# First layer of an adjacency kernel: product with the second weight after the sum over nodes, biases spread by DMA, other queues for x and the first piece of adj

## The chip, the cores and the metric

One core of a Trainium2 chip. TensorE (PE) multiplies, VectorE (DVE), ScalarE (ACT) and GpSimd (POOL) do the elementwise work, SyncE (SP) only issues transfers. SP and ACT each have a DMA queue of their own; q1 is SP's and q10 is ACT's. The metric is the time of one execution on the device in microseconds; less is better.

## The reference

x is 4096 nodes x 128 features, adj is 4096 x 4096, all float32. adj holds no negative value, and few of its entries are not zero.

```
# layer 0: at most 350 entries a row are kept; here no row has more
T    = tanh(adj * adj)                  # where adj > 0
h2   = tanh(x @ W_proj + b_proj)
feat = relu(T @ (h2 @ W_gcn) + b_gcn)
x    = layernorm(x + feat)
# layer 1
pos  = (adj > 0) @ x ;  neg = (adj < 0) @ x
y    = [pos, neg] @ node_weight + node_bias * diag(adj)
y   += (adj @ x) @ edge_weight + edge_bias * diag(adj)
x    = layernorm(x + y)
```

## The kernel before

The eight chunks of a layer are 512 rows of adj each. A chunk has eight halves of 512 columns (four blocks of 128). Each half goes through the same steps: DMA brings it in rows (four quarters make a piece of two halves, 2 MB), DVE transposes it by 32 x 32 squares into a_cols (L581, helper `turn`), and in layer 0 POOL squares three quarters of it (L354), ACT the rest (L515), ACT takes the tanh (L520), and PE adds four products of 128x512 to the accumulator acc (L913). There are four slots for halves; a slot comes free when PE has used it.

The work is written out by hand as one program for each engine, in order, with semaphores between them. Every engine takes its own list strictly in that order.

Ahead of the first chunk stands a head, the list USES, which makes the operand `rhs` = tanh(x W_proj + b_proj) W_gcn of 4096 nodes in eight groups of 512 nodes. A group is a "turn" (PE transposes x, L876, DVE copies it out of PSUM, L591), a "hid" (PE multiplies with W_proj, one product of 128x512, L881; ACT adds the bias and takes the tanh, L483), and a "rhs" (PE multiplies with W_gcn, four products of 128x128, L887; DVE, L593, or ACT, L488, copies it out). The groups are interleaved over six PSUM banks. EARLY names the places of DVE's list in the head at which the first halves of adj are transposed. ACT's list has the eight tanhs ahead of its first square (L515) of adj.

x comes in five parts of 4, 4, 8, 8 and 8 blocks (X_PARTS), each in four quarters of partitions: SP's queue brings the first two quarters of every part (L365), ACT's queue the other two (L457). Both queues have piece 0 of adj between parts 3 and 4. From group 2 on, ACT issues one quarter of the later pieces of adj after each tanh of the head (L460).

After a chunk, ACT empties acc into z_t with bias b_gcn and relu (L496), and PE transposes z_t back to rows (L898, `turn_to_rows`) between the first and second half of the next chunk. DVE adds x (L645) and normalises (L602 to L633), and ACT and POOL split the result in a high and a low part for layer 1.

Layer 1 uses for each block a product with adj (L922) and two with the mask adj > 0 (L923, L924). In its first chunk PE spreads the three bias rows over the partitions by products with a row of ones (L960 to L962) and DVE copies them out (L718).

## Time and profile before

| | us |
|---|---|
| median of three runs (621.15 to 621.41) | 621.28 |
| the profiled execution | 622.29 |
| its span, first to last instruction | 620.5 |
| PE busy in the span | 603.0 |
| DVE busy | 475.7 |
| ACT busy | 415.7 |
| POOL busy | 186.7 |

The span is what the trace covers; the profiled execution's own time has 1.8 us more around it. Its time is 1.0 us above the median of the other runs. Busy times of engines overlap.

### The profile page before, as it was taken

What the parts mean: (1) busy time and instruction counts of PE and PEld (TensorE: products, weight loads), DVE (VectorE), ACT (ScalarE), POOL (GpSimd) and SP (SyncE); (2) the same over time, 40 slices, a digit from 0 to 9 for tenths busy, and PEclk for the clock granted to TensorE, in tenths of its full rate; (3) what the DMA queues carried; (4) which work ended last, traced back from release to release, by engine and by line L of the source; (5) the groups of instructions that cost most, each with busy time, mean ns of one, the idle gap of its engine ahead of it and who ended that gap; (6) DMA issues with size and microseconds to landing.
All of it is one profiled execution on the core that took longest, in us unless ns stands there. A gap on an engine that the chain in (4) does not pass through costs nothing.

```text
span 620.5 us, 5693 instructions
## 1 busy us (share of the span) xinstructions
PE 603.0 (97%) x1966; PEld 342.3 (55%) x1966; DVE 475.7 (77%) x703; ACT 415.7 (67%) x293; POOL 186.7 (30%) x79
## 2 busy tenths in 40 slices
PE   7799999999999999999999999999999999999994
PEld 5544444444444444555655655655655656558993
DVE  2676979788887979986697696796786886877735
ACT  2378686868687686548784883983883874856850
POOL 0387697978879697000000000000000000000000
PEclk9899999999999999999999999999999999999998
DMA  8999999999999980048889398486595684883000
GB/s 235 336 347 347 330 282 315 270 328 287 324 281 298 315 197 0 1 135 229 219 250 252 97 246 232 127 243 188 154 250 154 186 248 125 230 232 96 2 18 18
DMA packets 141181, 130.65 MB, mean 211 GB/s; under 512 B 9443, under 2 KB 141158, under 8 KB 141158
## 3 DMA queue, kind: packets, MB, share of 16 engines
q1 hardware_dynamic: 74982, 66.22, 38.4%
q10 hardware_dynamic: 66176, 64.17, 37.2%
q8 instruction: 9, 0.15, 0.1%
q14 instruction: 14, 0.11, 0.1%
HBM read 128.27 MB, written 2.10 MB: 210 GB/s over the span
## 4 chain that ended last, share of the span: by engine, by line
PE 94%; DMA 2%; ACTq 2%; ACT 1%; DVE 1%; issue 0%
PE acc L913 35%; PE acc L922 33%; PE stage L924 10%; PE stage L923 10%; PE stage L922 2%; DMA x_rows<-in_x_dram 2%; PE to_rows L932 1%; PE to_rows L933 1%; ACTq L457 1%; ACTq L460 1%; PE to_rows L898 1%; PE stage L881 1%; ACT a_cols L520 0%; PE to_cols L887 0%; ACT a_cols L515 0%
## 5 line engine op out<-in xcount | busy, mean ns | idle before, releaser
L581 DVE STREAM_TRANSPOSE a_cols<-a_rows 128x2048 f32<-128x2048 f32 x128 | 294.6, 2306 | 90.8 <-PE stage L924 55.1
L922 PE MATMUL acc<-a_cols,x_rows 128*128 128x512 f32 (+1 forms) x512 | 248.1, 566 | 0.0
L913 PE MATMUL acc<-a_cols,rhs 128*128 128x512 f32 x512 | 221.4, 593 | 1.3 <-ACT a_cols L520 1.3
L923 PE MATMUL stage<-masks,x_hi 128*128 128x512 f32 (+1 forms) x288 | 208.5, 724 | 0.0
L354 POOL TENSOR_TENSOR a_cols<-a_cols 128x1536 f32<-128x1536 f32 x64 | 175.2, 2746 | 63.5 <-DVE a_cols L581 62.9
L913 PEld LDWEIGHTS acc<-a_cols,rhs 128*128 128x128 f32 x512 | 96.6, 190 | 120.4 <-issue 120.4
L520 ACT ACTIVATE a_cols<-a_cols 128x2048 f32<-128x2048 f32 x64 | 122.3, 1912 | 50.6 <-POOL a_cols L354 49.4
L536 ACT ACTIVATE a_rows<-a_rows 128x4096 f32<-128x4096 f32 x32 | 116.0, 3624 | 26.4 <-DVE a_cols L581 13.3
L539 ACT ACTIVATE a_rows<-a_rows 128x4096 f32<-128x4096 f32 x32 | 115.9, 3623 | 1.0
L924 PE MATMUL stage<-masks,x_lo 128*128 128x512 f32 (+1 forms) x288 | 106.7, 370 | 0.0
L922 PEld LDWEIGHTS acc<-a_cols,x_rows 128*128 128x128 f32 x512 | 94.0, 189 | 20.1 <-issue 0.5
L924 PEld LDWEIGHTS stage<-masks,x_lo 128*128 128x128 f32 x288 | 54.5, 189 | 55.4 <-issue 53.7
L923 PEld LDWEIGHTS stage<-masks,x_hi 128*128 128x128 f32 x288 | 54.3, 188 | 55.7 <-issue 53.9
L711 DVE TENSOR_SCALAR masks<-a_cols 128x2048 fp32r<-128x2048 f32 x64 | 79.0, 1234 | 2.2
L548 ACT COPY z_t<-acc 128x512 f32<-128x512 f32 x7 | 4.1, 585 | 65.1 <-PE stage L924 65.1
L515 ACT ACTIVATE a_cols<-a_cols 128x512 f32<-128x512 f32 x64 | 39.6, 618 | 5.9 <-issue 3.7
L922 PE MATMUL stage<-a_cols,x_rows 128*128 128x256 f32 x64 | 19.1, 380 | 0.0
L347 POOL TENSOR_TENSOR x_lo<-x_rows,x_hi 128x512 fp32r<-128x512 f32 x8 | 11.2, 1403 | 22.5 <-ACT x_hi L502 22.5
L483 ACT ACTIVATE early<-stage,b_col 128x512 f32<-128x512 f32 x7 | 4.8, 687 | 16.1 <-PE stage L881 10.0
L661 DVE COPY sm_t<-stage 128x512 f32<-128x512 f32 x7 | 4.8, 691 | 11.6 <-PE stage L924 11.6
L591 DVE COPY early<-stage 128x512 f32<-128x512 f32 x5 | 3.4, 690 | 11.3 <-PE stage L876 11.3
L932 PE MATMUL to_rows<-w_pne,z_t 128*128 128x128 f32 x60 | 11.7, 276 | 0.0
(84 smaller groups left out, 234.1 us busy)
## 6 DMA issues: line engine op xcount, KB each, us to landing
a_rows<-in_adj_dram SPq DMA_DIRECT2D x120, 512.0 KB, 8.9
a_rows<-in_adj_dram ACTq DMA_DIRECT2D x120, 512.0 KB, 10.0
out_dram<-n_rows SPq DMA_DIRECT2D x28, 64.0 KB, 8.4
x_rows<-in_x_dram SPq DMA_DIRECT2D x6, 128.0 KB, 4.2
x_rows<-in_x_dram ACTq DMA_DIRECT2D x6, 128.0 KB, 5.5
x_rows<-in_x_dram SPq DMA_DIRECT2D x4, 64.0 KB, 2.3
x_rows<-in_x_dram ACTq DMA_DIRECT2D x4, 64.0 KB, 2.7
diag<-in_adj_dram SPq DMA_DIRECT2D x16, 1.0 KB
```

Of the source, the lines that this page charges most:

```text
L354: nc.gpsimd.tensor_tensor(part, part, part, ALU.mult).then_inc(squared_pool, 1)
L515: nc.scalar.activation(rest, rest, ACT.Square).then_inc(squared_act, 1)
L520: nc.scalar.activation(a_cols[:, hs, :, :], a_cols[:, hs, :, :], ACT.Tanh)\
L536: nc.scalar.activation(piece, piece, ACT.Sign, accum_out=signs[:, bass.ds(col, 1)])\
L539: nc.scalar.activation(piece, piece, ACT.Relu, scale=-1.0, accum_out=negs[:, bass.ds(col, 1)]).then_inc(counted, 1)
L581: nc.vector.transpose(half_out(hs), half_in(s, h % HALVES)).then_inc(turned[layer], 1)
L711: nc.vector.tensor_scalar(masks[:, hs, :, :], a_cols[:, hs, :, :], 0.0, None, ALU.is_gt)\
L913: last = nc.tensor.matmul(acc[parity][:], rhs[:, b, :], a_cols[:, h % HSLOTS, k, :], start=(b == 0), stop=(b == BLOCKS - 1))
L922: nc.tensor.matmul(sums, x_rows[:, b, :], cols, start=(b == 0), stop=(b == BLOCKS - 1))
L923: nc.tensor.matmul(sums_m, x1_hi[:, b, :], mask, start=(b == 0), stop=False)
L924: return nc.tensor.matmul(sums_m, x1_lo[:, b, :], mask, start=False, stop=(b == BLOCKS - 1))
L932: nc.tensor.matmul(rows[:, k, :], blk(z_t, at + k), w_pne[:, 2, :], start=True, stop=False)
```

## The change

Layer 0 is computed as (T h2) W_gcn in place of T (h2 W_gcn).

- The "rhs" steps of the head go: eight times four products of 128x128, and the copies after them. The operand of the big products is h2 itself.
- The "hid" step changes sides: PE now has the transposed x as the stationary operand and W_proj as the moving one, four products of 128x128 in place of one of 128x512, so that h2 comes out in rows. DVE adds the bias on the way out of PSUM (it lies along the free axis now), and ACT takes the tanh in place in SBUF.
- `turn_to_rows` becomes `project`: the four transposes of z_t by the identity become four products of z_t with W_gcn.
- ACT only copies acc to z_t. The bias b_gcn and the relu move behind the projection, to DVE: one addition, and one maximum with the addition of x.
- All biases come spread over the 128 partitions by DMA. The three bias products of layer 1 and their copy go, and one small addition on DVE is new.
- SP's queue brings all of x but two quarters of part 0, then W_gcn and its bias, and then its half of pieces 1 to 3. ACT's queue brings the four quarters of piece 0 right after its two quarters of x. W_gcn was ACT's.
- EARLY is [("turn", 7), ("hid", 6)]: the first half of adj is transposed ahead of the copy of turn 7, the second ahead of hid 6.

```diff
-    EARLY = [("turn", 7), ("rhs", 4), ("rhs", 6)]
+    EARLY = [("turn", 7), ("hid", 6)]
...
         for k in range(GROUPS):
-            USES += hids[k:k + 1] + rhss[max(k - 2, 0):max(k - 1, 0)] + turns[k + 2:k + 3]
-        USES += rhss[GROUPS - 2:]
+            USES += hids[k:k + 1] + turns[k + 2:k + 3]
...
-            for part in range(1, X_FIRST):
-                load_x(part)
-            load_piece((0, 0), 0)
-            for part in range(X_FIRST, len(X_PARTS)):
-                load_x(part)
+            sp.dma_start(b_proj_bc, b_proj.partition_broadcast(P)).then_inc(proj_loaded, 16)
+            for part in range(1, len(X_PARTS)):
+                load_x(part, range(QUARTERS))
+            sp.dma_start(w_pg[:, 1, :], w_gcn).then_inc(gcn_loaded, 16)
+            sp.dma_start(b_gcn_bc, b_gcn.partition_broadcast(P)).then_inc(gcn_loaded, 16)
...
+            for q in range(QUARTERS):
+                load_quarter((0, 0), 0, q)
+
+            for g in range(GROUPS):
+                act.wait_ge(stage_dve, count_of("hid", g))
+                nc.scalar.activation(h2[:, g * TILES:(g + 1) * TILES, :], h2[:, g * TILES:(g + 1) * TILES, :], ACT.Tanh)\
+                    .then_inc(hid_ready, 1)
+                if g >= 2:
+                    load_quarter((0, 0), g // 2, ACT_QUARTERS[g % 2])
...
-                nc.scalar.activation(by_tile(z_t[:]), by_set(acc[parity][:]), ACT.Relu, bias=b_col[:, 1:2])\
-                    .then_inc(z_ready, 1)
+                nc.scalar.copy(by_tile(z_t[:]), by_set(acc[parity][:])).then_inc(z_ready, 1)
...
+                    nc.vector.tensor_tensor(h2[:, g * TILES:(g + 1) * TILES, :],
+                                            bank_of(n).rearrange("p (b f) -> p b f", f=F), to_all(b_proj_bc, TILES),
+                                            ALU.add).then_inc(stage_dve, 1)
...
-                    nc.vector.tensor_tensor(to_rows[:], to_rows[:], rows, ALU.add).then_inc(y_ready, 1)
+                    nc.vector.tensor_tensor(to_rows[:], to_rows[:], to_all(b_gcn_bc, TILES), ALU.add)\
+                        .then_inc(biased, 1)
+                    dve.wait_ge(biased, c + 1)
+                    nc.vector.scalar_tensor_tensor(out=to_rows[:], in0=to_rows[:], scalar=0.0, in1=rows, op0=ALU.max,
+                                                   op1=ALU.add).then_inc(y_ready, 1)
...
-                    last = nc.tensor.transpose(to_rows[:, k, :], z_t[:, k * P:(k + 1) * P], ident[:])
+                    last = nc.tensor.matmul(to_rows[:, k, :], blk(z_t, k), w_pg[:, 1, :], start=True, stop=True)
...
-                        nc.tensor.matmul(stage[0][:, 0:F], ones[0:1, :], b_row[:, 0, :], start=True, stop=False)
-                        nc.tensor.matmul(stage[0][:, 0:F], ones[0:1, :], b_row[:, 1, :], start=False, stop=True)
-                        nc.tensor.matmul(stage[0][:, F:2 * F], ones[0:1, :], b_row[:, 2, :], start=True, stop=True)\
-                            .then_inc(bias_staged, 1)
```

PE's list before, from turn 6 of the head to the first chunk (early holds the transposed x and the tanh of the hidden layer):

```order
L876 MATMUL stage<-ident,x_rows 128x128 x4
L881 MATMUL stage<-early,w_pg 128x512
L887 MATMUL to_cols<-w_pg,early 128x128 x4
L876 MATMUL to_rows<-ident,x_rows 128x128 x4
L881 MATMUL stage<-early,w_pg 128x512
L887 MATMUL stage<-w_pg,early 128x128 x4
L881 MATMUL stage<-early,w_pg 128x512
L887 MATMUL stage<-w_pg,early 128x128 x4
L887 MATMUL to_cols<-w_pg,early 128x128 x4
L887 MATMUL to_rows<-w_pg,early 128x128 x4
L913 MATMUL acc<-a_cols,rhs 128x512 x32
```

PE's list of the change at the same place (L863 is the turn, L869 the hid):

```order
L863 MATMUL to_rows<-ident,x_rows 128x128 x4
L869 MATMUL stage<-w_pg,feat_t 128x128 x4
L863 MATMUL stage<-ident,x_rows 128x128 x4
L869 MATMUL stage<-w_pg,feat_t 128x128 x8
L897 MATMUL acc<-a_cols,h 128x512 x32
```

The last rows ahead of the big products were four rounds of L887; now they are the two last hids.

DVE's list before, from the copy of turn 6 on:

```order
L591 COPY early<-stage 128x512
L581 STREAM_TRANSPOSE a_cols<-a_rows 128x16x4x32
L591 COPY early<-to_rows 128x512
L581 STREAM_TRANSPOSE a_cols<-a_rows 128x16x4x32
L593 COPY rhs<-stage 128x512 x2
L581 STREAM_TRANSPOSE a_cols<-a_rows 128x16x4x32
L593 COPY rhs<-to_cols 128x512
L593 COPY rhs<-to_rows 128x512
```

DVE's list of the change at the same place (L567 copies a turn, L571 adds the bias to a hid, L559 transposes adj):

```order
L567 COPY feat_t<-to_rows 128x512
L571 TENSOR_TENSOR h<-stage,b_lent 128x512
L559 STREAM_TRANSPOSE a_cols<-a_rows 128x16x4x32
L567 COPY feat_t<-stage 128x512
L559 STREAM_TRANSPOSE a_cols<-a_rows 128x16x4x32
L571 TENSOR_TENSOR h<-stage,b_lent 128x512 x2
L559 STREAM_TRANSPOSE a_cols<-a_rows 128x16x4x32 x11
```

Before, no tanh of the head stood behind a transpose of adj other than through the copy of turn 7; now the additions of hid 6 and 7, from which ACT takes its last two tanhs, stand behind both early transposes.

SP's list before:

```order
L365 DMA x_rows<-in_x_dram 32x4x128 x2
L373 DMA w_pg<-in_L_gnn_W_proj_dram 128x128
L374 DMA b_col<-in_L_gnn_b_proj_dram 128x1
L365 DMA x_rows<-in_x_dram 32x4x128 x2
L365 DMA x_rows<-in_x_dram 32x8x128 x4
L369 DMA a_rows<-in_adj_dram 32x16x256 x2
L365 DMA x_rows<-in_x_dram 32x8x128 x2
L369 DMA a_rows<-in_adj_dram 32x16x256 x62
```

SP's list of the change:

```order
L361 DMA x_rows<-in_x_dram 32x4x128 x2
L370 DMA w_pg<-in_L_gnn_W_proj_dram 128x128
L371 DMA b_lent<-in_L_gnn_b_proj_dram 128x128
L361 DMA x_rows<-in_x_dram 32x4x128 x4
L361 DMA x_rows<-in_x_dram 32x8x128 x12
L374 DMA w_pg<-in_L_gnn_W_gcn_dram 128x128
L375 DMA bias_bc<-in_L_gnn_b_gcn_dram 128x128
L365 DMA a_rows<-in_adj_dram 32x16x256 x62
```

SP now issues twice as many transfers of x, none of them behind a piece of adj.

## Rows read from the trace of the kernel before

**Rows 1.** The page: busy times, and the chain's shares.
```profile
PE 603.0 (97%) x1966; PEld 342.3 (55%) x1966; DVE 475.7 (77%) x703; ACT 415.7 (67%) x293; POOL 186.7 (30%) x79
...
PE acc L913 35%; PE acc L922 33%; PE stage L924 10%; PE stage L923 10%; PE stage L922 2%; DMA x_rows<-in_x_dram 2%; PE to_rows L932 1%; PE to_rows L933 1%; ACTq L457 1%; ACTq L460 1%; PE to_rows L898 1%; PE stage L881 1%; ACT a_cols L520 0%
```

**Rows 2.** The chain that ended last, 0 to 64 us: start, us, what.
```profile
7.66 12.36 DMA x_rows<-in_x_dram
...
24.63 0.86 PE stage L881 x2
25.49 0.89 PE stage L887 x8
...
32.88 1.92 ACT a_cols L520
...
34.93 27.70 PE acc L913 x64
62.64 0.44 PE to_rows L898 x4
```

**Rows 3.** The timeline, 0 to 45 us: start, us, engine, line, operation, idle before.
```profile
20.16 0.63 PE L876 MATMUL stage<-ident,x_rows 128*128 128x128 f32 x4 [2.90 <-DMA x_rows<-in_x_dram]
...
20.82 0.69 DVE L591 COPY early<-stage 128x512 f32<-128x512 f32 x1 [2.83 <-PE stage L876]
...
21.43 2.30 DVE L581 STREAM_TRANSPOSE a_cols<-a_rows 128x2048 f32<-128x2048 f32 x1
...
22.29 0.69 ACT L483 ACTIVATE early<-stage,b_col 128x512 f32<-128x512 f32 x1 [5.20 <-PE stage L881]
...
23.82 2.75 POOL L354 TENSOR_TENSOR a_cols<-a_cols 128x1536 f32<-128x1536 f32 x1 [22.20 <-DVE a_cols L581]
...
27.86 0.62 ACT L515 ACTIVATE a_cols<-a_cols 128x512 f32<-128x512 f32 x1
...
28.52 1.91 ACT L520 ACTIVATE a_cols<-a_cols 128x2048 f32<-128x2048 f32 x1
28.52 3.64 ACTq L460 DMA_DIRECT2D a_rows<-in_adj_dram  x2
...
30.57 3.67 PE L913 MATMUL acc<-a_cols,rhs 128*128 128x512 f32 x8 [0.65 <-ACT a_cols L520]
```

**Rows 4.** DMA from 6 to 8 us: queue, packets, MB, share of 16 engines.
```profile
q1 hardware_dynamic: 549, 0.27, 49.4%
q10 hardware_dynamic: 514, 0.25, 45.7%
```

**Rows 5.** The same from 16 to 18 us.
```profile
q1 hardware_dynamic: 499, 0.32, 60.6%
q10 hardware_dynamic: 495, 0.28, 55.2%
```

**Rows 6.** The same from 20 to 22 us.
```profile
q1 hardware_dynamic: 349, 0.35, 55.0%
```

**Rows 7.** The same from 10 to 12 us.
```profile
q1 hardware_dynamic: 280, 0.28, 57.3%
```

**Rows 8.** Stretches: us, busy of PE, PEld, DVE, ACT, POOL, then granted clock, DMA, GB/s.
```profile
20.00:25.00 5.00, 4.84 (x20) 3.74 (x21) 3.24 (x3) 1.27 (x2) 1.19 (x1) 0.66 1.10 348
```

**Rows 9.** The timeline around the three bias products of layer 1.
```profile
263.86 0.40 PE L924 MATMUL stage<-masks,x_lo 128*128 128x512 f32 x1
...
264.09 1.02 PE L922 MATMUL acc<-a_cols,x_rows 128*128 128x512 f32 x2
...
265.18 0.40 PE L924 MATMUL stage<-masks,x_lo 128*128 128x512 f32 x1
...
266.37 1.12 PE L922 MATMUL acc<-a_cols,x_rows 128*128 128x512 f32 x2
```

**Rows 10.** The timeline of one norm of layer 0.
```profile
64.98 0.67 DVE L645 TENSOR_TENSOR to_rows<-to_rows,x_rows 128x512 f32<-128x512 f32 x1
...
80.28 2.31 DVE L581 STREAM_TRANSPOSE a_cols<-a_rows 128x2048 f32<-128x2048 f32 x1 [0.87 <-PE acc L913]
```

More of the change, by code:

```diff
@@ L125, in build, with to_all @@
         var, y2v, rstd_ps = (to_cols[:, CH - k * TILES:CH - (k - 1) * TILES] for k in (1, 2, 3))
+        b_proj_bc, b_edge_bc = (b_lent[:, k, :] for k in range(2))
+        b_gcn_bc, b_node_bc = (bias_bc[:, k, :] for k in range(2))
+        def to_all(bias, tiles):
+            return bias.unsqueeze(1).to_broadcast([P, tiles, F])
         last_acc = [acc[LAST[2]], stage[0]]
@@ L296, in build @@
         GROUPS = BLOCKS // TILES
-        turns, hids, rhss = ([(kind, g) for g in range(GROUPS)] for kind in ("turn", "hid", "rhs"))
+        turns, hids = ([(kind, g) for g in range(GROUPS)] for kind in ("turn", "hid"))
         USES = turns[:2]
         for k in range(GROUPS):
-            USES += hids[k:k + 1] + rhss[max(k - 2, 0):max(k - 1, 0)] + turns[k + 2:k + 3]
-        USES += rhss[GROUPS - 2:]
-        by_dve = [k == "turn" or (k == "rhs" and g not in (1, 3)) for k, g in USES]
+            USES += hids[k:k + 1] + turns[k + 2:k + 3]
         HEAD = [stage[0][:], stage[1][:], stage[2][:], stage[3][:], to_cols[:],
@@ L309, in count_of @@
         def count_of(kind, g):
-            n = USES.index((kind, g))
-            return sum(by_dve[:n + 1]) if by_dve[n] else n + 1 - sum(by_dve[:n + 1])
-        def emptied(eng, n):
-            if by_dve[n]:
-                eng.wait_ge(stage_dve, count_of(*USES[n]))
-            else:
-                eng.wait_ge(stage_act, count_of(*USES[n]))
+            return USES.index((kind, g)) + 1
         def g_tiles(eng, body):
@@ L362, in _, with load_x @@
         def _(sp):
-            def load_x(g):
-                for q in SP_QUARTERS:
-                    sp.dma_start(x_of(g, q), x_in(g, q)).then_inc(x_loaded[g], 16)
+            def load_x(part, quarters):
+                for q in quarters:
+                    sp.dma_start(x_of(part, q), x_in(part, q)).then_inc(x_loaded[part], 16)
             def load_piece(rows, s):
@@ L876, in _ @@
                         last = nc.tensor.transpose(bank[:, k * P:(k + 1) * P], x_rows[:, g * TILES + k, :], ident[:])
-                elif kind == "hid":
+                else:
                     if g == 0:
@@ L880, in _, with project @@
                     pe.wait_ge(stage_dve, count_of("turn", g))
[L881 to L885 removed]
                     for k in range(TILES):
[L887 to L888 removed]
+                        last = nc.tensor.matmul(bank[:, k * P:(k + 1) * P], blk(feat_t, g * TILES + k),
+                                                w_pg[:, 0, :], start=True, stop=True)
                 last.then_inc(staged, 1)
[L891 removed]
+            def project(chunk):
                 c = chunk[0]
                 pe.wait_ge(z_ready, c + 1)
+                if is_first(c):
+                    pe.wait_ge(gcn_loaded, 32)
                 if not is_first(c):
@@ L1039, in g_contract @@
                         pe.wait_ge(g_split, n + 1)
-                        parts = [(g_cols, rhs)] + [(g_gt, g_pos), (g_lt, g_neg)] * layer
+                        parts = [(g_cols, h2)] + [(g_gt, g_pos), (g_lt, g_neg)] * layer
                         for k, (cols, operand) in enumerate(parts):
```

106 lines of the change are left out of this document (40 added, 66 removed).

## The prediction

> **What bounds the kernel now.** I read the page first: the busy times, and the chain's shares, show that PE works through 603.0 of the 620.5 us and that nearly all of the chain is PE's big products [rows 1]. So two things count: what PE does in the long stretch, and when that stretch begins. The chain in order of time says where it begins. From 34.93 us on, PE's 64 product records of a chunk (32 products, two records each) follow without a gap, 27.5 us for 64, that is 0.43 us a record, and then the four transposes of z_t take 0.44 [rows 2]. The reader is to see that nothing else stands between two chunks. Ahead of 34.93 the chain is the head: 12.36 us of waiting for x from ACT's queue, then PE's turn of group 6 at 20.16, the hids and rhs rounds, and last the second tanh of adj, 1.92 us at 32.88 [rows 2, 3]. The first half's eight records began at 30.57 and need 8 x 0.43 = 3.4 us, so PE stood still for under a microsecond before the second half [rows 3]. As a measure of the head I take the moment at which an unbroken stream would have to begin: 34.93 - 3.4 = 31.5 us. Every microsecond by which this moment moves is a microsecond of the kernel, since PE never waits again to speak of.
>
> **The projection after the sum.** Per chunk, four transposes at 0.44 become four products of 128x128 with W_gcn. The same shape stands in the head as L887, two records a product: 0.89 for four [rows 2]. It stands on PE's path between two halves of products, with nothing to hide it: 8 x (0.89 - 0.44) = +3.6 us. Bounds: the eight records at the spacing of 128 columns in the unbroken stream (a quarter of 0.43) give 0.86, so +3.4; with 0.1 us more a chunk, should PE wait for a new kind of weights, +4.4. I take 3.6.
> The Trainium skill ("TensorE: Matmul & The Clock Gate", Terms) says that transpose mode makes fp32 four times faster. By that rule, a product would cost four times a transpose, and the term would be 8 x 3 x 0.44 = 10.6 us; the trace's two rows say twice, and the measured row decides.
>
> **The bias products.** From the last L924 ahead of them to the next L922 there are 266.37 - 265.18 = 1.19 us, where one round earlier the same pair is 264.09 - 263.86 = 0.23 apart [rows 9]. They stood on PE's path and go: 1.19 - 0.23, -0.95 us. The wait for the weights of layer 1 stays at the same place; it had no idle time before it. The lower bound is 0.7, if the next product starts no earlier by its weight load.
>
> **DVE, ACT and POOL in the long stretch.** ACT's relu becomes a copy of the same size: nothing. DVE gets one more pass over 512 columns in each chunk, like L645 with 0.67 us [rows 10]. After the norm DVE comes to a transpose at 80.28 for which it waited 0.87 us for PE [rows 10]. That idle time covers 0.67, and the projection gives it another 0.45 by making PE's period longer. Cost nothing; if the cover were gone, what comes late is the square and the tanh of the seventh half, and PE would lose up to 0.7 in each of seven chunks.
>
> **The head: when the data is there.** In the changed kernel SP's queue brings 4096 packets of 512 bytes up to the end of x: 256 for its part 0, 128 for W_proj, 128 for the spread bias, 512 for part 1 and three times 1024. ACT's queue brings 256, and 2048 packets of 1 KB for piece 0, right behind. The DMA rows show how two queues share. With 512-byte packets on both, 549 and 514 go in 2 us, 530 a microsecond together [rows 4]; with 1 KB packets 350 together [rows 6]; and with mixed sizes, 499 and 495 [rows 5]. So they take turns by packets, not by bytes: beside a queue of 1 KB packets, x gets a third of the bytes. The first stretch with adj is slower, 280 packets of q1 in 2 us against 349 later [rows 6, 7]; over both queues and some 4 us I count 1.0 us for it. From 3.0 us (part 0 is then done on both queues) 2048 pairs take 2048 x (1/530 + 1/350) = 9.7, plus 1.0: piece 0 is over at 13.7. SP then has 1792 packets left, 3.4 us at 530: 17.1, and landed about 1 us later, 18.1. The same arithmetic on the kernel before (3840 small packets, 2048 large ones, and some 700 large ones with which SP's queue was ahead) gives 20.1, where part 4 landed at 20.02 [rows 2]. So part 4 comes 2 us earlier than before, but part 2 comes late: 3.0 + 1.0 + 1792 x 4.74 ns + 1 = 13.5. Bounds for part 4: 17 and 20, the upper one if one queue alone with small packets is slower than two.
>
> **The head: what follows it.** With part 2 at 13.5, PE has five rounds of a turn (0.63) and a hid (0.89) until hid 5 is over: 7.6 us, 21.1, three microseconds behind the landing of part 4, so PE's rounds end last and not the transfer. Then the order shown above holds on DVE and ACT: addition of hid 5 (0.7), transpose (2.3), copy of turn 7 (0.7), transpose (2.3), two additions (1.4), then ACT's last tanh (0.69), square (0.62) and tanh (1.91) [rows 3], 10.6, and 0.3 for semaphores: PE starts at 32.1. That is 0.6 later than 31.5, although four rhs rounds left PE's tail: before, they lay beside DVE's transposes and ACT's squares and weren't what ended last, while now both early transposes stand ahead of ACT's last two tanhs.
> The transfer issues that held ACT up before its second square (3.64 us for two [rows 3]) stood behind four 512 KB quarters of ACT's queue that had not landed, by my count from the issues; with the quarters of pieces 1 to 3 issued at the tanhs as above I estimate three now, and take no stall; with it, up to 1.0 more.
>
> **The clock.** Before, PE was idle for 2.90 us until 20.16, and the stretch after it has a granted clock of 0.66, that is 3.4 of 5 us at the lower of the two levels [rows 3, 8]. The L887 round in it took about twice 0.89. In the changed kernel PE has nothing to do between hid 7 (about 26.0, behind the copy of turn 7) and 32.1, twice as long as that gap. So the first half's products begin at 1.2 GHz: a loss between nothing and 1.7 us (half of 3.4); I take 1.2. The waits for parts 1 and 2 are gaps of some 4 us as well, and what is slow in the five rounds costs 0 to 1.2; I take 0.6.
> Head in all: 0.6 + 1.2 + 0.6 = +2.4, with bounds of -0.5 (part 2 a microsecond earlier, no slow clock) and +4.5 (all of it at its worst).
>
> **The sum.** 622.29 (the profiled execution, its span of 620.5 and 1.8 around it) + 3.6 - 0.95 + 2.4 = 627.3. The median of the runs shown is 1.0 below that execution: 626.3.
>
> **The rivals.**
> First, the head costs nothing: part 2 lands earlier than by turns of packets, and PE's clock stays up. Then 626.3 - 2.4 = 623.9, down to 623.4 at the bound of the head, and to 622.5 if the projection's weight loads hide fully and the bias products give 1.2. For it: 2 us less transfer before part 4. Against it: an idle PE of 6 us.
> Second, the added pass of DVE does surface: up to 7 x 0.7 = +4.9, 631.2. For it: DVE's norm has POOL's square and ACT's tanh of the later halves behind it, and PE behind these. Against it: the 0.87 us of idle time [rows 10], every chunk.
> Third, on the other side: the transfers run well ahead of my count, so that x and piece 0 have both landed by 14 us. PE's rounds would then run from part 1 on and end at 16.5, PE's stream would start at 16.5 + 11 = 27.5, 4.0 before 31.5, and with 3.6 - 0.95 for the rest the kernel would be at 619.9. It decides from 28.9 on downwards for no change, from 27.6 for a gain that can be measured. It needs 4.3 MB in 11 us, 390 GB/s, where the trace shows 348 with both queues full [rows 8].
> Fourth, a transpose is four times cheaper than a product where both run in a tight stream: 626.3 + 7.0 = 633.3. It is the page's rule in this kernel, and rows 2 speak against it.
>
> **How the numbers follow.** My forecast 0.72, the first rival 0.15, the second 0.06, the third 0.05, the fourth 0.02. The time is that of the forecast, 626.3 us. Its own bounds (head from +0.5 to +4.5, projection 3.4 to 4.4) reach from 624 to 629; towards the first rival I go to 623.3, and to the second not at all, so 0.1 to 0.15 is left outside. Faster by more than 0.2%, about what a measurement of this kernel can tell from no change, is the third rival alone, 0.05; within 0.2% (up to 622.5) the edge of the first and a bit of the third, 0.06; slower 0.89.
>
> **What would show it.** The projection: 0.86 to 0.9 us between two products of different chunks where 0.44 stood. The bias products: no gap between L924 and L922 in the second half of layer 1's first chunk. The transfers: equal counts of packets on q1 and q10 from 4 to 13 us with half the bytes on q1; the turn of group 2 at 13 to 14, that of group 6 at 19 to 20 and right behind a hid. The order: the first product of adj at 32 or later, a granted clock under 1 in the 5 us that follow. The prediction is wrong if the first product starts before 30, if it starts at full clock, or if waits of PE for ACT's tanh appear after the first chunk.

## The result: 637.49 us, 2.5% slower

| | before | after |
|---|---|---|
| median, us | 621.35 (621.15 to 621.95, 4 runs) | 637.49 (635.94 to 638.52, 4 runs) |
| the profiled execution, us | 622.29 | 635.94 |
| its span, us | 620.5 | 634.1 |

The ratio is 1.0251, 95% interval 1.0237 to 1.0265: 15.6 us, where the prediction had 5.0 and its range ended at 629.0. The direction was right and the size was not. In the spans the difference is 13.6.

**Where it went.** The page of after, busy times and the chain's shares, against [rows 1]:

```profile
PE 602.9 (95%) x1976; PEld 345.7 (55%) x1976; DVE 481.9 (76%) x713; ACT 413.6 (65%) x291; POOL 186.5 (29%) x79
...
PE acc L897 33%; PE acc L906 33%; PE stage L908 9%; PE stage L907 9%; PE stage L906 2%; DMA x_rows<-in_x_dram 2%; ACTq L452 1%; PE to_rows L882 1%; PE to_rows L916 1%; PE to_rows L917 1%; SPq L361 1%; DVE a_cols L559 1%; ACT a_cols L498 1%; PE stage L869 0%; PE to_cols L869 0%
```

PE is as busy as before in a span 13.6 us longer: the time is standing still, not work. The chain in order of time says where (start, us, what), against [rows 2]:

```profile
7.64 11.15 DMA x_rows<-in_x_dram
...
18.84 1.12 PE stage L863 x4
...
27.65 0.69 DVE h L571
...
35.19 1.79 ACTq L452
...
43.60 1.79 issue
...
46.40 3.79 ACTq L452
...
52.95 20.84 PE acc L897 x48
73.79 0.89 PE to_rows L882 x8
74.68 27.47 PE acc L897 x64
102.15 0.89 PE to_rows L882 x8
```

The first chunk ended at 62.64 and now ends at 73.79: the head lost 11.15 us. From there on a chunk takes 27.47 + 0.89 where it took 27.5 + 0.44, and nothing else stands between two chunks. So outside the head the change costs what was written down, and almost all that was not foreseen lies before 53 us. The timeline of that stretch, against [rows 3]:

```profile
2.60 15.66 SPq L361 DMA_DIRECT2D x_rows<-in_x_dram  x16
...
15.11 1.12 PE L863 MATMUL stage<-ident,x_rows 128*128 128x128 f32 x4 [9.90 <-DMA x_rows<-in_x_dram]
...
18.84 1.12 PE L863 MATMUL stage<-ident,x_rows 128*128 128x128 f32 x4 [0.91 <-DMA x_rows<-in_x_dram]
...
34.56 2.41 ACTq L452 DMA_DIRECT2D a_rows<-in_adj_dram  x1
...
37.69 5.18 ACTq L452 DMA_DIRECT2D a_rows<-in_adj_dram  x2
...
39.74 5.45 PE L897 MATMUL acc<-a_cols,h 128*128 128x512 f32 x8 [7.33 <-ACT a_cols L498]
...
45.64 7.10 PE L897 MATMUL acc<-a_cols,h 128*128 128x512 f32 x16 [0.45 <-ACT a_cols L498]
46.05 4.14 ACTq L452 DMA_DIRECT2D a_rows<-in_adj_dram  x2
```

PE stood still for 9.90 us until part 1 of x was there, at 15.11. The prediction had put this wait at some 4 us. Part 2, forecast for 13.5, was used at 18.84. The DMA view from 6 to 8 us (queue, packets, MB, share), against [rows 4], where q1 had 549 packets:

```profile
q10 hardware_dynamic: 267, 0.27, 47.6%
q1 hardware_dynamic: 95, 0.04, 28.5%
```

And from 8 to 10 us:

```profile
q10 hardware_dynamic: 374, 0.37, 92.8%
q1 hardware_dynamic: 139, 0.06, 20.4%
```

These are not equal counts: SP's queue, which has x, gets a quarter of the packets. Stretches of after (columns as in [rows 8]):

```profile
10.00:15.00 5.00, 0.00 (x0) 0.00 (x0) 0.00 (x0) 0.00 (x0) 0.00 (x0) 0.50 1.16 232
15.00:20.00 5.00, 3.98 (x18) 3.69 (x19) 1.39 (x3) 0.63 (x1) 0.00 (x0) 0.50 1.22 241
...
25.00:30.00 5.00, 3.94 (x36) 3.75 (x34) 4.92 (x6) 1.91 (x4) 0.00 (x0) 1.00 1.13 205
...
35.00:40.00 5.00, 0.26 (x1) 0.29 (x2) 2.11 (x1) 2.72 (x3) 1.17 (x1) 0.50 1.10 347
```

The granted clock is at the lower level, 1.2 GHz, in the idle stretch from 10 us and still when PE works from 15 on, and again after PE's idle time from 32.4 on. The last column gives 205 to 241 GB/s from 10 to 30 us, and 347 from 35 on.

### The profile page after: what moved, and what is told of

The parts are those of the page before. It is cut to its first block, busy times and chain, and to the rows that moved or that the text cites. A ratio compares the mean times of both kernels' runs of the same rounds, so it can differ in the third digit from the quotient of the medians.

```text
span 634.1 us, 5713 instructions
## 1 busy us (share of the span) xinstructions
PE 602.9 (95%) x1976; PEld 345.7 (55%) x1976; DVE 481.9 (76%) x713; ACT 413.6 (65%) x291; POOL 186.5 (29%) x79
## 4 chain that ended last, share of the span: by engine, by line
PE 92%; DMA 2%; DVE 2%; ACTq 1%; ACT 1%; SPq 1%; issue 1%
PE acc L897 33%; PE acc L906 33%; PE stage L908 9%; PE stage L907 9%; PE stage L906 2%; DMA x_rows<-in_x_dram 2%; ACTq L452 1%; PE to_rows L882 1%; PE to_rows L916 1%; PE to_rows L917 1%; SPq L361 1%; DVE a_cols L559 1%; ACT a_cols L498 1%; PE stage L869 0%; PE to_cols L869 0%
## 5 line engine op out<-in xcount | busy, mean ns | idle before, releaser
L559 DVE STREAM_TRANSPOSE a_cols<-a_rows 128x2048 f32<-128x2048 f32 x128 | 294.4, 2305 | 95.2 <-PE stage L908 54.2
L897 PE MATMUL acc<-a_cols,h 128*128 128x512 f32 x512 | 223.4, 596 | 8.0 <-ACT a_cols L498 8.0
L897 PEld LDWEIGHTS acc<-a_cols,h 128*128 128x128 f32 x512 | 97.2, 191 | 128.5 <-issue 128.5
L906 PEld LDWEIGHTS acc<-a_cols,x_rows 128*128 128x128 f32 x512 | 94.1, 189 | 20.1 <-issue 0.5
L467 ACT ACTIVATE h<-h 128x512 f32<-128x512 f32 x8 | 5.0, 630 | 27.0 <-DVE h L571 27.0
L343 POOL TENSOR_TENSOR x_lo<-x_rows,x_hi 128x512 fp32r<-128x512 f32 x8 | 11.2, 1405 | 23.2 <-ACT x_hi L480 23.2
L567 DVE COPY feat_t<-stage 128x512 f32<-128x512 f32 x6 | 4.1, 680 | 16.9 <-PE stage L863 16.9
L863 PE MATMUL stage<-ident,x_rows 128*128 128x128 f32 x24 | 5.1, 351 | 10.8 <-DMA x_rows<-in_x_dram 10.8
```

Source lines behind the costliest of these rows:

```text
L343: nc.gpsimd.tensor_tensor(rows_at(x1_lo, rows), rows_at(x_rows, rows), rows_at(x1_hi, rows).bitcast(f32), ALU.subtract).then_inc(lo_ready, 1)
L559: nc.vector.transpose(half_out(hs), half_in(s, h % HALVES)).then_inc(turned[layer], 1)
L897: last = nc.tensor.matmul(acc[parity][:], h2[:, b, :], a_cols[:, h % HSLOTS, k, :], start=(b == 0), stop=(b == BLOCKS - 1))
L906: nc.tensor.matmul(sums, x_rows[:, b, :], cols, start=(b == 0), stop=(b == BLOCKS - 1))
```

## The experiments

Ratios are against the kernel before on the same chip, with 95% intervals; four runs each where nothing else is said. As us I give ratio minus one, times 622.

### e1: the change, with the transfers of before

```diff
-            for part in range(1, len(X_PARTS)):
-                load_x(part, range(QUARTERS))
+            for part in range(1, 4):
+                load_x(part, SP_QUARTERS)
+            load_piece((0, 0), 0)
+            load_x(4, SP_QUARTERS)
```

and the same four lines on ACT with its own quarters.

> The changed kernel with the transfers of before: every part of x and piece 0 split between the two queues (SP the quarters 0 and 1, ACT 2 and 3), piece 0 between parts 3 and 4. All else as changed. Theory A (the 11 us that the head lost are the new use of the queues: SP's x and ACT's piece 0 go to the same half of the partitions, 0 to 63, and share what one half takes): part 4 lands near 20 us as before, the stream of big products starts at 33 to 34, and the time is 626, my forecast without its transfer term. Theory B (the loss is the new order of DVE's and ACT's lists, with both early transposes ahead of the last two tanhs): 633 or more, hardly better than the changed kernel.

Measured: 632.17 us, 1.0152 [1.0117, 1.0188]. It lies between the two theories, nearer to B: the queues carry 6.2 us of the 15.6, and 9.4 stay, more than a projection and a reordered head were said to cost. Its timeline:

```profile
22.00 1.08 PE L871 MATMUL to_rows<-ident,x_rows 128*128 128x128 f32 x4 [4.89 <-DMA x_rows<-in_x_dram]
...
32.92 3.12 ACTq L454 DMA_DIRECT2D a_rows<-in_adj_dram  x2
34.97 31.62 PE L905 MATMUL acc<-a_cols,h 128*128 128x512 f32 x67 [5.38 <-ACT a_cols L506]
```

With the queues and the order of x of before, the turn of group 6 still comes at 22.00 and not at 20.16 [rows 3]. That is taken up below (e8 to e11).

### e2: the kernel before, with the new queues alone

Both loops over the parts of x are replaced: SP brings all quarters of parts 1 to 4, ACT the four quarters of piece 0.

> The kernel before with only the new use of the queues: SP brings all of x but two quarters of part 0, ACT brings the four quarters of piece 0 behind the second weight. Layer 0 is computed as before. Theory A: part 1 of x lands at 13 to 15 us in place of 6, PE's clock is low in the head, and the time is 621 + 8 to 11 = 629 to 632. Theory B: 621 to 623.

Measured: 635.46 us, 1.0198 [1.0161, 1.0236]: 12.3 us from the queues alone, in a kernel with none of the other edits. Its timeline has the same late start:

```profile
14.07 1.11 PE L871 MATMUL stage<-ident,x_rows 128*128 128x128 f32 x4 [8.87 <-DMA x_rows<-in_x_dram]
...
40.60 5.11 PE L908 MATMUL acc<-a_cols,rhs 128*128 128x512 f32 x8 [3.16 <-ACT a_cols L515]
```

This kernel has no spread bias, and PE's wait for part 1 is still 8.87 us, so the queues alone are enough for it. The costs do not add up edit by edit: the same use of the queues costs 12.3 us here and 6.2 in the changed kernel. Which of the other delays cover the difference, no run shows.

### e3: ACT's quarters of piece 0 in the order 2, 3, 0, 1

```diff
-            for q in range(QUARTERS):
+            for q in (2, 3, 0, 1):
```

> The changed kernel, but ACT brings the quarters of piece 0 in the order 2, 3, 0, 1, so that at first it writes partitions 64 to 127 while SP writes part 1's quarters 0 and 1. Theory A (halves of the partitions): SP's first small transfers run at the full rate of small packets until they come to quarters 2 and 3; part 1 lands some us earlier than at 15, and the time is 1 to 5 us under that of the changed kernel. Rival (the 1 KB packets of adj crowd out the 512-byte packets of x wherever they go): no change, 637.

Measured: 637.91 us, 1.0246 [1.0211, 1.0281], part 1 used at 14.94. Nothing changed: to which partitions piece 0 goes first does not explain the late part 1.

### m1 and m2: the transfers by themselves

m1 has transfers of 512 KB only, in packets of 1 KB (adj) or 512 bytes (x), three at a time on each queue, into chosen quadrants of 32 partitions.

> No kernel of the task: only transfers, in eight phases, each over before the next begins, the output is zeros. A transfer is 512 KB in 1 KB packets of adj (or in 512-byte packets of x) to 32 partitions. Phases: SP alone to quadrant 0; SP to 0 and ACT to 2 from other columns; SP to 0 and ACT to 1; both to 0; SP to 0 and ACT to 2 from the same columns; x by SP alone to 0; x by SP to 0 and adj by ACT to 2; x by SP to 0 and adj by ACT to 0. Theory A (a half of the partitions takes some 205 GB/s, quadrants 0 and 1 are one half): 205, 350, 205, 205, 350 GB/s, then about 235, 320 and 205, the last with few packets of x. Rival (a quadrant is the limit, not a half): phase 3 at 350. Rival (the source columns set it): phases 3 and 4 at 350, phase 5 at 205. Rival (a single queue is the limit): every phase with both queues at 350.

The DMA view of m1 with adj to quadrant 0 by one queue and to quadrant 2 by the other, 16 to 20 us:

```profile
DMA packets 1355, 1.35 MB, mean 339 GB/s; under 512 B 32, under 2 KB 1355, under 8 KB 1355
```

and with both to quadrant 0, 44 to 48 us:

```profile
DMA packets 826, 0.81 MB, mean 203 GB/s; under 512 B 32, under 2 KB 826, under 8 KB 826
q10 hardware_dynamic: 418, 0.41, 56.9%
q1 hardware_dynamic: 408, 0.40, 56.5%
```

Quadrants 0 and 1 give 214 GB/s, and one queue to quadrant 0 alone 209. So the half with the partitions 0 to 63 takes some 203 to 214 GB/s of adj, whether one queue sends it or two, and both halves at once give 339; the other half alone was not measured. The Trainium skill ("SBUF — State Buffer", Door 1: The DMA port swizzle) says that partitions 32 further on share a quadrant's ports and that those 64 further on have others; these runs agree. In the changed kernel each queue brings one quadrant after the other, and two quadrants in turn lie in one half, where before SP always had one half and ACT the other; the 205 to 241 GB/s above fit that. How much of the 6.2 us it carries beside the shares below, no run tells apart.

m1 also has x from one queue beside adj from the other, in the same half, 96 to 100 us:

```profile
q1 hardware_dynamic: 887, 0.45, 69.1%
q10 hardware_dynamic: 386, 0.38, 49.9%
```

Here x moves more packets than adj, where I had expected few, and the counts come to 551 and 548 from 100 to 104 us. Small packets are not what starves x.

m2 puts short transfers of x beside adj's 512 KB.

> Transfers only, in nine phases, the output is zeros. SP brings x in 512-byte packets, in transfers of 4 packets a partition (64 KB) or 8 (128 KB) to 32 partitions; ACT brings 512 KB transfers of adj. Phases: 4 a partition alone; beside adj to the other half of the partitions; beside adj to the same half; 8 a partition beside adj to the other half; to the same half; alone; alone with the quadrants 0 and 2 in turn; the same beside adj to 0, 2, 0; and x to all 128 partitions in each transfer, alone. Theory C (turns are taken by transfer, not by packet: a small transfer of x gets one turn for each large one of adj): in phases 2 and 3 SP's queue gets a fourth of ACT's packets or less, in phases 4 and 5 about half. Theory D (turns go by packet whatever the size): equal counts, and the late part 1 in the changed kernel has another cause. In the seventh phase and the last one both halves of the partitions are written by one queue: if a half is the limit and not the queue, the last one runs over 235 GB/s.

With transfers of 64 KB on q1, 23 to 26 us:

```profile
q10 hardware_dynamic: 626, 0.62, 97.5%
q1 hardware_dynamic: 143, 0.06, 13.6%
```

With transfers of 128 KB on q1, 36 to 39 us:

```profile
q10 hardware_dynamic: 492, 0.49, 68.8%
q1 hardware_dynamic: 390, 0.19, 29.2%
```

In m1, with 512 KB of adj on both sides, the counts were nearly equal. So the share of a queue goes by the length of its transfers, not by packets one for one. Short transfers beside adj in the other half of the partitions had somewhat more (198 to 563 packets with 64 KB, 390 to 492 with 128 KB) than in the same half (143 to 626, and 262 to 550), though the stretch from 36 us takes in the start of its phase. The Trainium skill ("DMA: Bandwidth & Descriptors", Queues, rings and completion order) says that an engine drains a bundle of descriptors from one queue before it turns to the next. If what the profile counts as packets are these descriptors, the bundles here grow with the transfer. Microsecond by microsecond from 22 to 28, q1 moved 135, 8, 123, 12, 10 and 125 packets, and one of its transfers has 128: a turn is about a whole transfer. The prediction had the right idea of turns and the wrong unit.

### e7: the change, with piece 0 in transfers of 128 KB

```diff
-                load_quarter((0, 0), 0, q)
+                for r in range(0, ROWSETS, 4):
+                    act.dma_start(quarter_of(0, q)[:, r:r + 4, :], quarter_in((0, 0), 0, q)[:, r:r + 4, :])\
+                        .then_inc(first_loaded, 16)
```

> The changed kernel, but ACT brings each quarter of piece 0 in four transfers of 128 KB in place of one of 512 KB (128 packets of 1 KB each, so that they are as long in packets as SP's transfers of part 1). Which queue brings what, and to which partitions, is unchanged. Theory C (turns are taken by transfer, so long transfers on ACT's queue crowd out the short ones of x): part 1 of x lands at 8 to 11 us in place of 15, and the time is 2 to 5 us under that of the changed kernel, 633 to 635. Rival (only the halves of the partitions matter): part 1 still lands after 14 us, the time is 637 within 1.

Measured: 634.32 us, 1.0203 [1.0172, 1.0233], 3.0 us better than the change. Its timeline:

```profile
10.42 1.11 PE L869 MATMUL stage<-ident,x_rows 128*128 128x128 f32 x4 [5.21 <-DMA x_rows<-in_x_dram]
...
16.71 0.85 PE L869 MATMUL stage<-ident,x_rows 128*128 128x128 f32 x4 [3.47 <-DMA x_rows<-in_x_dram]
```

Its DMA view from 6 to 8 us, where the change had 267 and 95:

```profile
q10 hardware_dynamic: 329, 0.30, 65.4%
q1 hardware_dynamic: 369, 0.17, 42.1%
```

Same bytes, same queues, same order, only shorter transfers beside x: SP's queue gets its half of the packets (part 1's 64 KB and adj's 128 KB are 128 packets each, so the length that counts is the one in packets), part 1 comes 4.7 us earlier and part 2 by 2.1. This shows the mechanism in the kernel itself. It gives back 3.0 of the 6.2 us. The total rate stays at 209 to 232 GB/s from 6 to 14 us (e1: 231 to 316), which fits the halves of the partitions as the rest, but nothing was run to show it.

### e4 and e5: the clock, and the order on DVE, on top of e1

e4 adds six idle products of 128x512 behind the last hid, in PE's gap:

```diff
+            def fill(count):
+                for _ in range(count):
+                    nc.tensor.matmul(acc[1][:], ones[:], x_rows[:, 0:TILES, :].rearrange("p t f -> p (t f)"),
+                                     start=True, stop=True)
+
+            fill(6)
```

> e1 (the changed kernel with the transfers of before), and PE computes six idle products of 128x512 into the unused accumulator between the last hid of the head and the first product of adj, where it stood still for 5.4 us; their output is used by nobody. Theory (the low clock at the start of the stream costs 2.6 to 2.9 us of the 6 us that the head of e1 lost): the granted clock is 1 from 35 us on and the time is 2 to 3 us under that of e1, 629.5. Rival (the low clock comes from somewhere else, or the idle products delay the first real one): no gain or a loss.

Measured: 630.86 us, 1.0146 [1.0122, 1.017]. From 26.8 us on the granted clock is 1, and the first eight records take 3.67 us and not 5.4. But the second half was then late, behind 3.60 us of ACT's transfer issues. The time is not clear of e1's: the clock was kept up, and its gain, expected at 2 to 3 us, did not come through.

e5 makes EARLY [("turn", 6)], so that the first transpose lies in DVE's idle time ahead of that copy, and the second behind the last addition.

> e1 with EARLY = [(turn, 6)]: DVE transposes the first half of adj ahead of the copy of turn 6, where e1's DVE stood still for 5.3 us, and the second half after the whole head. Theory (ACT's last two tanhs stand behind both transposes, 4.6 us of DVE): the first product of adj starts at 31.8 in place of 35.0, and the time is 2 to 4 us under e1, 628 to 630. Rival (piece 0 lands too late for that place, and the wait moves to DVE): within 1 us of e1.

Measured: 630.45 us, 1.0119 [1.0093, 1.0144]. The first product starts at 32.65 where e1 has 34.97, and the second half waits for ACT, whose two issues now take 6.20 us. The 2.0 us below e1 are within the two intervals. Both traces show the same thing: behind each delay of the head stands the next one, and the prediction's "take no stall" for ACT's issues was wrong in both.

### e6 and e8: all of it together, and even lists

e6 is e1 with e4's and e5's edits, and with the first two issues for the next chunk moved behind ACT's second tanh of adj:

```diff
-                    if h % HALVES == HALVES - 1 and chunk is not LAST:
+                    late = chunk == (0, 0, 0) and h == 1
+                    if h % HALVES == HALVES - 1 and chunk is not LAST and not late:
...
+                    if late:
+                        load_piece(rows_of(0, next_of(chunk)), 0)
```

> e1 with all three mends of the head: the six idle products of e4, the order of e5 (first half of adj transposed ahead of turn 6, the second behind the head), and the two transfer issues for the next chunk behind ACT's second tanh, as in b2. Theory (what e1's head lost is the list order, the low clock and the stall behind the issues): nearly all of the head's loss comes back and the projection's 3.6 less 0.95 stays: before plus 2.7 to 4.5, a ratio of 1.004 to 1.007. Rival (there is a further loss that I don't see): a ratio over 1.010.

Measured: 630.03 us, 1.014 [1.0079, 1.0201]. Its four times are two near 627 and two near 633, so the ratio decides nothing. The profiled one (626.97) has a stream from 33.23 on that ends the chunk at 64.87, 2.2 us behind before, with part 4 of x landed at 22.2.

e8 is e6 with W_gcn and the spread b_gcn on ACT again, ahead of part 1, so that both queues have as many packets before it.

> e6, with the second weight and its spread bias back on ACT's queue ahead of part 1 of x, 256 packets there as SP has 256 for the first weight and its bias. In e6 part 4 of x landed at 22.2 us, 2 us later than before. Theory (ACT's queue comes to its long transfers of adj a microsecond sooner than SP's and crowds out SP's half of x): part 4 lands at 20 to 20.7, and the head costs nothing any more, a ratio to before of 1.004 to 1.006 from the projection alone. Rival (the spread bias on SP's queue is what delays it): part 4 still lands at 22.

Measured: 628.45 us, 1.0103 [1.0072, 1.0135], but part 4 landed at 23.25, later still. The theory that uneven lists alone delay it fell. From 4 to 6 us, where before moves 248 GB/s and e1 208, e8 moves:

```profile
DMA packets 291, 0.14 MB, mean 68 GB/s; under 512 B 27, under 2 KB 291, under 8 KB 291
```

The more biases are spread by DMA in the head, the less everything moves around them: none in before, one in e1, two in e8. Such a transfer reads one row of 512 bytes 128 times. It takes 4.2 us to land in e1 and 5.0 and 5.8 in e8, where a weight of the same size takes 2.2 to 2.5 before.

### e9 and e10: W_proj in the place of the spread bias

```diff
-            sp.dma_start(b_proj_bc, b_proj.partition_broadcast(P)).then_inc(proj_loaded, 16)
+            sp.dma_start(b_proj_bc, w_proj).then_inc(proj_loaded, 16)
```

e9 is this on e1, e10 on the change. In both the bias of the hidden layer is replaced by other numbers.

> The changed kernel with the transfers of before (SP two quarters, ACT two quarters of every part of x, piece 0 between parts 3 and 4), but what fills the tile of b_proj is W_proj, 128 rows of 512 bytes from 128 different places, in place of the one row of 512 bytes read 128 times: same size, same number of packets, same place in SP's list. The bias of the hidden layer is so left out and replaced by other numbers. The theory (reading one row 128 times holds the DMA engines up, to about 208 GB/s from 4 to 6 us): with a flat transfer the rate from 4 to 6 us is back at some 245 GB/s, part 4 of x has landed by 20.5 us instead of 21.9, the first product of adj starts 1.2 to 1.8 us earlier than 34.97, and the ratio is 1.011 to 1.013 against 1.015. The rival (it is the mere number of transfers and packets in SP's list): landing at 21.9 and a ratio of 1.015.

> The changed kernel as it is, with its own queues, but W_proj in place of the spread row of b_proj (the bias of the hidden layer is so replaced by other numbers). The theory (the repeated row slows the transfers by about 1.5 to 2 us): PE's first turn on part 1 is at 13 to 13.6 us where it was 15.1, ratio 1.021 to 1.023 against 1.025. The rival (only the share that short transfers get beside long ones counts): part 1 stays at 14.9 to 15.2 and the ratio at 1.025.

Measured: e9 632.86 us, 1.0164 [1.0094, 1.0234]; e10 635.77 us, 1.0201 [1.0131, 1.0272]. In e9 the rate from 4 to 6 us is back (272 GB/s), but part 4 is used at 22.13, no earlier. In e10 part 1 is used at 14.28, 0.8 us earlier than in the change. Neither time is clear of that of the kernel it was made from. So the repeated row alone does not explain the two microseconds either: the slow stretch moved to 8 to 10 us, where ACT's queue was already at piece 0 (355 packets) and SP's short transfers of x got 155.

### e11 and e12: exactly the lists of before

Neither the repeated row nor the count alone explains the delay, so here both are undone at once. e11 is e1 with W_gcn on ACT again, and each bias of layer 0 as a column:

```diff
-            sp.dma_start(b_proj_bc, b_proj.partition_broadcast(P)).then_inc(proj_loaded, 16)
+            sp.dma_start(b_col[:, 0:1], b_proj.rearrange("(p a) -> p a", a=1)).then_inc(proj_loaded, 16)
...
+            act.dma_start(w_pg[:, 1, :], w_gcn).then_inc(gcn_loaded, 16)
+            act.dma_start(b_col[:, 1:2], b_gcn.rearrange("(p a) -> p a", a=1)).then_inc(gcn_loaded, 16)
```

In the place of the addition of the bias DVE has a copy of the same 0.69 us; the bias of the hidden layer is left out. e12 is the same with e6's three edits.

> The changed kernel with exactly the lists of transfers that the kernel before has up to the last part of x: W_gcn is ACT's again ahead of part 1, and each bias of layer 0 comes as a column of 128 x 4 bytes in place of the row spread over the partitions (the spread b_gcn follows at the end of SP's list). The bias of the hidden layer is left out: DVE's addition is a copy of the same size. If the lists explain the landing (theory): part 4 has landed at 20.0 to 20.7 and PE's turn 6 starts by 20.8, against 21.9 and 22.0 with one spread bias and an uneven list; the first product of adj starts at 33.0 to 33.8 and the ratio is 1.010 to 1.012. If it is the changed order of work on PE, DVE and ACT that delays it (rival): landing at 21.9 again and 1.015.

> The same lists, and all that helped apart: one early transpose ahead of the copy of turn 6, six idle products in PE's gap, and the first two issues for the next chunk behind ACT's second tanh of adj (the bias of the hidden layer left out, as above). With part 4 landed by 20.7 the stream of products starts so that the first chunk ends by 63.5 us, against 62.64 before and 64.87 without the even lists; with +3.6 for the projections and -0.7 for the bias products the ratio is 1.004 to 1.007: then the layer's new order costs little more than the projection. If the landing does not move: 1.010 or more.

Measured: e11 628.55 us, 1.0112 [1.009, 1.0134]. Its timeline:

```profile
20.15 1.09 PE L872 MATMUL to_rows<-ident,x_rows 128*128 128x128 f32 x4 [5.18 <-DMA x_rows<-in_x_dram]
...
31.08 2.69 ACTq L454 DMA_DIRECT2D a_rows<-in_adj_dram  x2
33.13 33.03 PE L906 MATMUL acc<-a_cols,h 128*128 128x512 f32 x72 [4.56 <-ACT a_cols L508]
```

The turn of group 6 starts at 20.15, the very place of before (20.16 [rows 3]). e12: 624.74 us (seven runs), 1.0038 [1.0025, 1.005], 2.4 us. But its profiled execution, the slowest of the seven (630.75; the others took 623.87 to 625.83, and the mean of all seven lies 3.4 us above before's), has the same lists as e11 and a late landing:

```profile
22.36 1.09 PE L875 MATMUL to_rows<-ident,x_rows 128*128 128x128 f32 x4 [3.39 <-DMA x_rows<-in_x_dram]
```

So the lists of before allow the early landing and do not secure it. With them the turn of group 6 started at 20.15 to 20.89 in four traces (before, b1, b2, e11) and at 22.36 in the fifth. With the spread bias, or with the uneven list of e9, it started at 22.00 to 23.39 in all six (e1, e4, e5, e6, e8, e9). That the lists matter is shown by this and by the time of e12 beside that of e6. That they explain all of the two microseconds is not shown, and what delayed e12's execution is open. The projections and the bias products together are 2.9 us by measured rows and runs. So by the ratio of e12, with the lists of before, the clock kept up and the issues out of ACT's way, the head is as short as before's, and the projection is what is left. The kernel before gains by such help too, though (b2 against b1, below: 1.9 us). Like for like, e12 against b2, the layer's new order costs 2.4 + 2.6 = 5.0 us, 3.6 of it projections and 1.4, good to about 1.1, the head.

### b1 and b2: what can be kept

b1 is the kernel before with layer 1's biases spread by DMA, without the three bias products.

> The kernel before with one part of the change alone: the biases of layer 1 come spread by DMA, the three bias products and their copy go, one addition of 128 columns is new. By the rows of the trace PE saves 1.19 - 0.23 us: 0.95 under before. Rival: nothing, because the wait for the transfers takes the place of the products.

Measured over twelve runs: 621.24 us, 0.9989 [0.9975, 1.0003]: -0.7, just inside what this can tell from nothing.

b2 is b1 with e6's late issues, and three idle products in PE's gap ahead of the turn of group 6.

> b1, and two edits in the head of the kernel before: three idle products of 128x512 in the gap in which PE waits for part 4 of x (2.9 us, after which its clock was at the lower level for 3.4 us), and the first two transfer issues for the next chunk stand behind ACT's second tanh of adj in place of ahead of its square. Expected: 0.95 from the biases, 1.5 from the clock, 0.9 from the issues, together 3.3 under before, 618. Rival: the clock falls anyway or part 4 is the limit, then 1 to 2 under before.

Measured: 619.53 us (five runs, 619.26 to 619.94), 0.9958 [0.9945, 0.9971]. It is faster than both kernels by more than its interval; 3.3 us under before were expected, and it is 2.6. Its timeline:

```profile
17.18 2.74 PE L874 MATMUL acc<-x_rows,ones 128*128 128x512 f32 x6
20.26 0.63 PE L886 MATMUL stage<-ident,x_rows 128*128 128x128 f32 x4 [0.34 <-DMA x_rows<-in_x_dram]
...
29.02 10.54 PE L923 MATMUL acc<-a_cols,rhs 128*128 128x512 f32 x24 [0.65 <-ACT a_cols L520]
```

PE has 0.34 us of idle time ahead of the turn in place of 2.90, the rounds behind it run at full clock, and adj's first product starts at 29.02 and not at 30.57 [rows 3].

## Why the prediction was wrong, step by step

The measured parts, by ratios times 622:

| part | shown by | us | predicted |
|---|---|---|---|
| eight projections | 0.89 against 0.44, eight times | +3.6 | +3.6 |
| bias products | b1 | -0.7 | -0.95 |
| head, with the lists of before | e11, less the two above | +4.1 | |
| spread bias and uneven lists ahead of part 1 | e1 less e11 | +2.5 | |
| x on SP's queue, piece 0 on ACT's | change less e1 | +6.2 | |
| head in all | | +12.8 | +2.4 |
| sum | | +15.7 | +5.0 |

The parts of the head are differences of ratios, and the half-widths of these ratios' intervals are 0.1 to 0.4%. So the 6.2 is good to about 2.4 us, and the 2.5 to about 2.6: for that part only the landings in the traces speak clearly. e2 shows that the order in which the parts are taken matters.

**The projection: right.** 0.89 us eight times, as the row of L887 gave it [rows 2]. The rule of the Trainium skill ("TensorE: Matmul & The Clock Gate", Terms), by which it would have been 10.6, does not hold for these shapes: the measured factor is 2 (0.89 against 0.44).

**The bias products: right by the rows.** b1's time alone would not tell the gain from nothing. Where they stood, the rows of after are now 0.23 apart:

```profile
278.66 0.40 PE L908 MATMUL stage<-masks,x_lo 128*128 128x512 f32 x1
...
278.89 1.02 PE L906 MATMUL acc<-a_cols,x_rows 128*128 128x512 f32 x2
```

**The added pass of DVE: right.** One more row of 0.67 us per norm [rows 10], and the profile lists no wait of PE from 64 us on:

```profile
76.13 0.67 DVE L626 TENSOR_TENSOR to_rows<-to_rows,bias_bc 128x512 f32<-128x512 f32 x1
...
76.83 0.70 DVE L629 SCALAR_TENSOR_TENSOR to_rows<-to_rows,x_rows 128x512 f32<-128x512 f32 x1
```

**When the data is there: wrong, and the step that failed.** The prediction said of the two queues that "they take turns by packets, not by bytes", from stretches in which both queues had long lists of transfers of like length or were moving from one kind to the other [rows 4 to 6]. By that, part 2 was to land at 13.5. m2 shows that a queue of 64 KB transfers beside one of 512 KB gets not one packet in two but one in four or five, and one of 128 KB one in two or three; e7 shows that even lengths give even counts again. That the same sum gave 20.1 for the kernel before, against 20.02, proved nothing for this case: there both queues had transfers of like length. By the prediction's own arithmetic part 1, the first 768 packets, would have landed at 3.0 + 1.0 + 768 x 4.74 ns + 1 = 8.6; it was used at 15.11. SP's queue moved 95 and 139 packets in 2 us there in place of 549, and PE's first wait is 9.90 us. The prediction knew of the spread bias as 128 packets like any others; the rates of e1, e8 and e9 from 4 to 6 us (208, 68 and 272 GB/s) show that it is not, though e9 and e10 also show that it is not all of the delay. How it and an uneven list work together is left open.

**What follows it: the durations right, the path longer.** Five rounds were priced at 7.6 us, plus 0.6 for the clock; from 18.84 to 27.6 they took 8.8. From there to the first product of adj there were to be 10.9; it took 12.1, of which 1.79 is ACT held up by its issues (chain, at 35.19). Without that stall e11 takes 10.2 us from DVE's step of hid 5 (22.98) to the first product (33.13).

**"I take no stall": wrong.** The issues at 34.56, 37.69 and 46.05 took 2.41, 5.18 and 4.14 us, and PE's stream is unbroken from 52.95 only. With x late, ACT issues its quarters of pieces 1 to 3 from 24.39 on, where before it began at 12.03. SP's twelve quarters stood in line in both kernels (its issues took 33.90 us before and 33.22 now). Why ACT is held up for longer is not shown; the traces show only that its issues follow each other faster.

**The clock: right in kind, too small.** Predicted were an idle PE ahead of the first product and a slow start: 1.2 us, at most 1.7. The eight records, which began at the lower level, took 5.45 where they need 3.44: 2.0. With the 0.9 of waits behind ACT's issues, PE's stream stands where one that began at 52.95 - 24 x 0.43 = 42.6 would, 11.1 behind the 31.5 of before.

So against the prediction's head of 2.4, 5.3 of the error of 8.7 is part 2 alone (18.84 against 13.5), 0.6 its slow rounds, 1.2 the tail, and 1.7 clock and issues behind the first product. The rest up to 11.2 is that the median is 1.55 above the profiled execution of after, where the prediction had subtracted 1.0 for that of before.

Of the rivals, none came: the head was far from free, DVE's pass stayed hidden, the transfers ran behind the count and not ahead of it, and the fourfold rule did not hold. That the kernel became slower would have come out of the projections alone; the sizes of the head were not foreseen.

## What to carry to other kernels

Before moving transfers between queues, count not bytes or packets but the length of the transfers on either side in each stretch: short transfers that something waits for must not run beside long ones that nobody needs yet, and if they must, cut the long ones up. Rows that are spread over partitions are better brought after what is waited for, though no run here tried just that. And when one wait of a head is taken away, look at once for the next one behind it (here the clock, then the list order on DVE, then the issues on ACT): the three edits together gave 4.6 us from e11 to e12, while e4 and e5 alone gave 0.4 and 2.0 on e1, neither clear of it.

## What the runs showed of the hardware

- Two queues share the DMA engines by the length of their transfers. Of 1 KB packets in 512 KB transfers beside another queue's packets: 418 to 408 against 512 KB of the same, 492 to 390 and 550 to 262 against 128 KB of 512-byte packets, 626 to 143 and 563 to 198 against 64 KB (m1, m2). Against 512 KB of 512-byte packets it was 386 to 887 at one time and 548 to 551 at another (m1).
- The partitions 0 to 63 take 203 to 214 GB/s in transfers of 1 KB packets from one queue or two, both halves 339 (m1).
- A row spread over 128 partitions by DMA takes 4.2 to 6.8 us to land in the head (e1, e8, after), where a flat transfer of the same 64 KB takes 2.2 to 2.9; beside ACT's long transfers a flat one took 6.4 too (e10). The total rate beside two of them falls to 68 GB/s (e8).
- ACT's instruction stream is held up by its own transfer issues: up to 6.20 us for two quarters of 512 KB (e5), where a single one took 0.32 in the same head.
- A product of 128x128 in float32 takes twice as long as a transpose of the same shape (0.89 against 0.44 for four, before and after).
